# A language-model tower on one core: the output biases from TensorE to VectorE, layer-norm rows among the gelus, one table load taken out, RMS factors five steps earlier

## The chip, the cores and the metric
The kernel runs on one core of a Trainium2 chip. Its time is the device time of one execution, in microseconds (us), as the median of several runs. Engines are named as in the profile: PE (TensorE, matmuls), PEld (its weight loads), DVE (VectorE), ACT (ScalarE), POOL (GpSimd), SP (SyncE, which issues most DMAs).

## The reference
64 sequences of 128 token ids, width 256. Cut to what matters:

```python
h = take(concat(quantize(tw_i * ts_i, bits_i)), ids)          # embedding, four tiers
x = layernorm(h)                                              # attention-like block on x
r = rms(x, norm1_w)
z, u, B, C, dt = split(r @ in_proj_w.T)                       # 512, 512, 16, 16, 8
u, B, C = silu(causal_conv4([u, B, C]) + conv_b)
B, C = B * rsqrt(sum(B*B) + 1e-6), C * rsqrt(sum(C*C) + 1e-6)
d = softplus(dt + dt_bias)
# for t in time: zs = (zs + d*(u*B - A*y)) / (1 + d*d*A); y = y + d*zs; out_t = y . C_t
y = (out + D_skip * u) * silu(z)
x2 = x + y @ out_proj_w.T + out_proj_b                        # first bias of the change
m = gelu(rms(x2, norm2_w) @ fc1_w.T + fc1_b)
h = h + x2 + m @ fc2_w.T + fc2_b                              # second bias of the change
h = h + int8_linear(layernorm(h))                             # one activation scale for all rows
```

## The kernel before
Three blocks follow each other. The first reads the whole table (81 MB) for the tiers' maxima and gathers the rows. The last is the int8 layer. The block between, where the change lies, works on 16 groups of 4 sequences (512 tokens) in 19 turns; turns 4 to 14 are one hardware loop, the others are written out. Each turn holds up to four stages of four different groups: `first` (group g: rows normalised, projected, the small projection of B, C and dt, the recurrence), `second` (group g-1: scores, scan output, gate, out projection), `third` (group g-2: the MLP, gelus 0 to 7) and `fourth` (group g-3: final layer norm and its maximum). The order on each engine is written out by hand in `pe_turn`, `act_turn`, `dve_turn`, `pool_turn`; semaphores join them.

What the steps below touch:
- **POOL** runs the recurrence, 64 steps of two dependent 128x32 instructions (L787, L789). It starts when X, the replicated and scaled d, is there: small projection on PE (L651), exp and ln on ACT (L669, L671), `dd` on DVE (L707), a DMA to memory and eight back (`sp_replicate`), then four activations (L762). Between the steps POOL also makes the norm factors of the next group and, after step `RMS_STEP`, the RMS factors of group g-1 (`pool_rms`, L1047 and L1049). In turn 1 these RMS factors stand behind the last step.
- **ACT** needs those factors for `act_rms_rows` (L1058, buffer xr), PE then transposes (L1064), ACT copies the result out (L1071, mT), and PE begins fc1 (L1091). The first gelu (L1101) lets fc2 (L1113) begin. Before the first gelu ACT has the silus of z (L924), the row copies (L637), the small projection's work with two table loads for exp and ln (L667, L684), and the gelu's own load.
- **PE** adds the biases: `pick` has ones in three rows, `bias3` holds each bias split in three bf16 parts, and a 128x512 bf16 matmul adds them to a bank (L1020 twice per turn ahead of the out projection, L1109 twice ahead of fc2). DVE makes the split in turn 0 (`dve_split_biases`).
- **DVE** after the keys, the inverse (L863) and the queries (L870) applies the masks (L987) to the scores that PE has just made (L976); PE's scan output (L997) waits for them.
- **ACT** makes xl, the layer-normed rows of group g-1 (L955), behind the last gelu and the utok copies (L945). DVE adds the out projection to it (L1032).

Of the kernel before, what the change touches and what calls it, by code (L numbers as in the profile page):

```python
# [36 lines left out]
G = 4  # L37
# [13 lines left out]
RMS_STEP = 52  # L51
# [36 lines left out]
def build(nc, a, out):  # L88
    with ExitStack() as ctx:
# [22 lines left out]
        bias3 = sb("bias3", [P, 2, 2 * D], BF16)  # L112
        pick = sb("pick", [P, P], BF16)
# [42 lines left out]
        LATE_WEIGHTS = ((w_fc1, "w_fc1"), (w_out, "w_out"), (w_fc2, "w_fc2"))  # L156
        OUT_B, FC2_B = 0, 1
# [313 lines left out]
        bias_in, halved, pick_cleared = sem("bias_in"), sem("halved"), sem("pick_cleared")  # L471
# [55 lines left out]
        seeded = signal("seeded", 2)  # L527
        h2_ready = signal("h2_ready", 2)
# [16 lines left out]

        def dve_split_biases(dve):
            whole = utok[:, 0:2, :]
            rest = utok[:, 2:4, :]
            dve.wait_ge(bias_in, 16)
            dve.tensor_copy(bias3[:], whole).then_inc(halved, 1)  # L550
            dve.wait_ge(halved, 1)
            dve.tensor_tensor(rest[64:P], whole[64:P], bias3[64:P], ALU.subtract).then_inc(halved, 1)
            dve.wait_ge(halved, 2)
            dve.tensor_copy(bias3[64:P], rest[64:P]).then_inc(halved, 1)
            dve.wait_ge(halved, 3)
            dve.tensor_tensor(rest[96:P], rest[96:P], bias3[96:P], ALU.subtract).then_inc(halved, 1)
            dve.wait_ge(halved, 4)
            dve.tensor_copy(bias3[96:P], rest[96:P]).then_inc(halved, 1)
# [124 lines left out]
        def act_small_rsqrt(act, g):  # L683
            act.preload_act_table_set("natural_log_exp_and_others")  # L684
            act.wait_ge(nrm_act.sem, nrm_act.at(g, 1))
            act.activation(nrm[:], bsq[:], ACT.Ln).then_inc(nrm_act.sem, 1)
            act.wait_ge(nrm_act.sem, nrm_act.at(g, 2))
            act.activation(nrm[:], nrm[:], ACT.Exp, scale=-0.5).then_inc(nrm_act.sem, 1)
# [268 lines left out]

        score_bank = (tb[0], tb[1], pj[2], pj[3])
# [54 lines left out]
        def pe_out(pe, g):  # L1013
            pe.wait_ge(m_ready.sem, m_ready.at(g))
            if since(g):
                pe.wait_ge(h2_ready.sem, h2_ready.at(g - 1))
            else:
                pe.wait_ge(halved, 5)
            for n in range(2):
                pe.matmul(sbk[n][:, :], pick[:], bias3[:, OUT_B, :], start=True, stop=False, skip_group_check=True)  # L1020
                for j in (2 * n, 2 * n + 1):
                    for f in range(UT):
                        if j == 0:
                            pe.wait_ge(yg_ready.sem, yg_ready.at(g, f + 1))
                        last = pe.matmul(sbk[n][:, (j % 2) * D:(j % 2 + 1) * D], sz[:, f, j * LEN:(j + 1) * LEN],  # L1025
                                         w_out[:, f, :], start=False, stop=(f == UT - 1), skip_group_check=True)
                last.then_inc(o_mm.sem, 1)

        def dve_x2(dve, g, n):
            dve.wait_ge(xl_ready.sem, xl_ready.at(g))  # L1030
            dve.wait_ge(o_mm.sem, o_mm.at(g, n + 1))
            dve.tensor_tensor(xl[:, 2 * n:2 * n + 2, :], sbk[n][:, :].rearrange("p (j c) -> p j c", j=2),  # L1032
                              xl[:, 2 * n:2 * n + 2, :], ALU.add).then_inc(x2_ready.sem, 1)
# [70 lines left out]
        def pe_fc2(pe, g, n):  # L1104

            if n == 0:
                pe.wait_ge(seeded.sem, seeded.at(g))
                for i in range(2):
                    pe.matmul(sbk[i][:, :], pick[:], bias3[:, FC2_B, :], start=False, stop=False,  # L1109
                              skip_group_check=True)  # L1110
# [10 lines left out]
        def dve_h2(dve, g):  # L1121
            for n in range(2):
# [109 lines left out]
        def act_turn(act):  # L1232
            def turn(g, first, second, third, fourth, nxt):
# [7 lines left out]
                if first:  # L1241
                    act_rows_T(act, g)
                if second:
                    act_silu_z(act, p, (3,))
                if third:
                    act_mlp_T(act, m)
# [4 lines left out]
                if first:  # L1251
                    act_small_silu(act, g)
                    act_small_dt(act, g)
                if first:
                    act_small_norm(act, g)
                    act_small_rsqrt(act, g)
                for n in range(FT):
# [6 lines left out]
                    if first and n == 3:  # L1264
                        act_rep(act, g, (1,))
                if second:
                    act_utok(act, p)
                if second:
                    act_layer_norm(act, p)
# [18 lines left out]
        def dve_turn(dve):  # L1288
            def turn(g, first, second, third, fourth, nxt):
# [16 lines left out]
                if not second and nxt:  # L1306
                    dve_bc(dve, g)
                    dve_split_biases(dve)
                    dve_first_steps(dve)
                if second:  # L1310
                    for hh in range(4):
# [31 lines left out]
        def pool_turn(pool):  # L1343
            def turn(g, first, second, third, fourth, nxt):
# [5 lines left out]
                if first and third:  # L1350
# [3 lines left out]
                elif first:  # L1354
                    pool_recurrence(pool, g, range(CL // 2 if second else DVE_STEPS, CL))
                if second and not (first and third):
# [6 lines left out]
        with nc.Block() as block:  # L1363
            @block.sync
            def _(sp):
                sp.dma_start(utok[:, 0:2, :], a["bias"].rearrange("p (i c) -> p i c", i=2)).then_inc(bias_in, 16)

# [21 lines left out]
            def _(dve):  # L1389
# [6 lines left out]
                dve.memset(pick[:], 0.0).then_inc(pick_cleared, 1)  # L1396
                dve.wait_ge(pick_cleared, 1)
                for r in (0, 64, 96):
                    dve.memset(pick[r:r + 1, :], 1.0)
# [313 lines left out]
```

## Time and profile before

| what | value |
|---|---|
| median of 3 runs | 1381.36 us (1380.7 to 1381.74) |
| the profiled execution's own time | 1378.95 us |
| its span, first to last instruction | 1377.1 us |
| busy in the span: PE, DVE, ACT, POOL | 1143.6, 1044.5, 804.8, 780.9 us |
| middle block | from about 175 to 1321 us |
| granted PE clock from 320 to 1223 us | 1.00 of full speed |

The span and the time of the same execution differ by 1.85 us, which lies around the span. In the page's slices PE is 9 tenths busy or more from about 310 us on to 1300 us, while no other engine is. A busy share is no proof of a bound, since PE's idle moments are short and come at fixed places of each turn, so the timelines of one turn are read.

### The profile page before, as it was taken

How to read it: one execution, taken by the hardware profiler on the slowest of the kernel's cores; microseconds unless marked ns; L12 is line 12 of the kernel's file. 1: busy time of each engine (PE TensorE's matmuls, PEld its weight loads, DVE VectorE, ACT ScalarE, POOL GpSimd, SP SyncE). 2: the span in 40 equal slices, each digit the busy share in tenths (PEclk: the TensorE clock that was granted, in tenths of full speed). 3: DMA queues.
4: the chain of work that ended last, by engine and by line, in shares of the span. 5: the costliest groups of instructions: out<-in, count | busy, mean ns of one | idle time of the engine just before them, and what ended most of it. 6: DMA issues, size and time to landing. Idle time of an engine off the chain costs nothing. (4 is left out here: it accounts for less than half of the span.)

```text
span 1377.1 us, 24832 instructions
## 1 busy us (share of the span) xinstructions
PE 1143.6 (83%) x7231; PEld 759.6 (55%) x7270; DVE 1044.5 (76%) x1764; ACT 804.8 (58%) x1288; POOL 780.9 (57%) x2326
## 2 busy tenths in 40 slices
PE   3980032488999999999999999999999999999857
PEld 1550021355766667565757575757666675757534
DVE  5988957756768787877888888887787877786178
ACT  4666433537475756657484847574757566552357
POOL 8880023372757575867667675767575858570000
PEclk9999996588999999999999999999999999999989
DMA  9999610000010000001010101010100000000015
GB/s 367 407 408 410 276 35 15 18 17 19 8 29 15 21 18 17 19 15 29 5 34 0 34 0 34 0 34 6 28 14 20 17 17 20 17 18 2 0 48 197
DMA packets 62082, 92.65 MB, mean 67 GB/s; under 512 B 9101, under 2 KB 54754, under 8 KB 57682
## 3 DMA queue, kind: packets, MB, share of 16 engines
q1 hardware_dynamic: 58386, 82.36, 16.8%
q0 software_dynamic: 3072, 8.39, 1.6%
q10 hardware_dynamic: 576, 1.31, 0.3%
q8 instruction: 23, 0.38, 0.1%
q14 instruction: 25, 0.20, 0.1%
HBM read 81.55 MB, written 10.49 MB: 67 GB/s over the span
## 5 line engine op out<-in xcount | busy, mean ns | idle before, releaser
L787 POOL TENSOR_TENSOR stp<-Gs,X 128x32 f32<-128x32 f32 x984 | 269.8, 274 | 259.0 <-ACT X L762 165.1
L789 POOL TENSOR_TENSOR Gs<-Gs,stp 128x32 f32<-128x32 f32 x984 | 274.3, 279 | 77.0
L641 PE MATMUL bank<-xT,w_in 128*128 128x512 f32 x512 | 239.8, 613 | 26.6 <-DVE uT L899 26.6
L1113 PE MATMUL bank<-w_fc,gl 128*128 128x256 f32 x1024 | 244.5, 382 | 10.7 <-ACT gl L1101 10.7
L1091 PE MATMUL bank<-mT,w_fc 128*128 128x512 f32 x512 | 238.7, 600 | 7.3 <-ACT mT L1071 7.3
L1113 PEld LDWEIGHTS bank<-w_fc,gl 128*128 128x128 f32 x1024 | 189.8, 190 | 69.5 <-issue 26.8
L641 PEld LDWEIGHTS bank<-xT,w_in 128*128 128x128 f32 x512 | 96.1, 195 | 129.5 <-issue 97.0
L885 ACT ACTIVATE uT<-bank,cols 128x512 f32<-128x512 f32 x64 | 47.9, 775 | 190.4 <-DVE sz L1011 155.1
L1091 PEld LDWEIGHTS bank<-mT,w_fc 128*128 128x128 f32 x512 | 95.8, 192 | 93.6 <-issue 86.9
L987 DVE TENSOR_TENSOR MT<-bank,causal 128x512 f32<-128x512 f32 x128 | 79.4, 682 | 85.4 <-PE bank L976 85.4
L1101 ACT ACTIVATE gl<-bank,cols 128x512 f32<-128x512 f32 x128 | 84.2, 682 | 98.9 <-PE bank L1113 94.2
L899 DVE SCALAR_TENSOR_TENSOR uT<-bank,cols,uT 128x500 f32<-128x500 f32 (+1 forms) x192 | 133.3, 735 | 2.3
L346 DVE TENSOR_TENSOR peak<-ring,peak 128x1536 f32<-128x1536 f32 (+2 forms) x67 | 115.2, 1720 | 7.9 <-ACT ring L248 6.2
L248 ACT ACTIVATE ring<-ring 128x3072 f32<-128x3072 f32 (+4 forms) x36 | 90.7, 2530 | 49.9 <-DMA ring<-in_table 49.9
L1025 PE MATMUL bank<-w_out,sz 128*128 128x256 f32 x512 | 116.5, 381 | 1.1 <-issue 0.3
L1025 PEld LDWEIGHTS bank<-w_out,sz 128*128 128x128 f32 x512 | 98.0, 191 | 19.5 <-issue 5.0
L863 DVE RECIPROCAL rm<-rm 128x1024 f32<-128x1024 f32 x16 | 104.7, 6543 | 0.0
L232 POOL DMA_INDIRECT h<-in_table,ids x64 | 82.0, 1281 | 19.4 <-issue 19.4
L762 ACT ACTIVATE X<-d_rep,cols 128x512 f32<-128x512 f32 x64 | 72.6, 1187 | 27.8 <-DMA d_rep<-d_rows 27.8
L286 PE MATMUL bank<-ts,hot 4*128 4x256 f32 x128 | 60.3, 648 | 19.6 <-ACT hot L259 14.1
L695 DVE SCALAR_TENSOR_TENSOR bc<-bank,cols,bc 128x127 f32<-128x127 f32 (+2 forms) x48 | 16.7, 348 | 72.4 <-ACT bc L661 71.3
L976 PE MATMUL bank<-Qf,Kf 32*128 32x64 f32 x2048 | 67.8, 282 | 3.1 <-DVE Qf L870 3.1
(184 smaller groups left out, 1868.5 us busy)
## 6 DMA issues: line engine op xcount, KB each, us to landing
ring<-in_table SPq DMA_DIRECT2D x31, 1536.0 KB
d_rep<-d_rows SPq DMA_DIRECT2D x128, 64.0 KB, 2.7
out<-res SPq DMA_DIRECT2D x16, 512.0 KB, 2.9
b_rep<-bc_rows SPq DMA_DIRECT2D x128, 32.0 KB, 1.8
c_rep<-bc_rows SPq DMA_DIRECT2D x128, 32.0 KB, 1.8
w_fc<-in_w_fc SPq DMA_DIRECT2D x2, 1024.0 KB, 8.8
ring<-in_table SPq DMA_DIRECT2D x2, 768.0 KB
w_in<-in_w_in ACTq DMA_DIRECT2D x1, 1088.0 KB
```

The source lines that it names most:

```text
L232: pool.indirect_dma_start(out=h[:, b * D:(b + 1) * D], out_offset=None, in_=table, in_offset=bass.IndirectOffsetOnAxis(ap=ids[:, b:b + 1], ...
L248: act.activation(ring[n % RING][0:np_, 0:nr, :], ring[n % RING][0:np_, 0:nr, :], ACT.Abs) \
L346: return dve.tensor_tensor(acc, ring[t][0:np_, r0:r0 + nr, :], acc, ALU.max)
L641: last = pe.matmul(dst, w_in[:, k, c0:c1], xT[:, k, :], start=(k == 0), stop=(k == KD - 1))
L787: pool.tensor_tensor(stp[:], Gs[:, t, ::-1, :], X2[:, t, :, :], ALU.mult).then_inc(rec.sem, 1)
L789: pool.tensor_tensor(Gs[:, t + 1, :, :], Gs[:, t, :, :], stp[:], ALU.add).then_inc(rec.sem, 1)
L863: dve.reciprocal(rm[:], rm[:]).then_inc(inverted.sem, 1)
L899: dve.scalar_tensor_tensor(acc[:, :, i:], ps[:, :, 0:LEN - i], c("u_tap", f * TAPS + TAPS - 1 - i), acc[:, :, i:], ALU.mult, ALU.add).then ...
L1025: last = pe.matmul(sbk[n][:, (j % 2) * D:(j % 2 + 1) * D], sz[:, f, j * LEN:(j + 1) * LEN], w_out[:, f, :], start=False, stop=(f == UT - 1 ...
L1091: last = pe.matmul(pj[n % 4][:, :], w_fc1[:, k, n * P:(n + 1) * P], mT[:, k, :], start=(k == 0), stop=(k == KD - 1))
L1101: act.activation(gl[n % LEAD][:], pj[n % 4][:, :], ACT.Gelu_apprx_tanh, bias=c("fc1_bias", n)) \
L1113: last = pe.matmul(sbk[j // 2][:, (j % 2) * D:(j % 2 + 1) * D], gl[n % LEAD][:, j * LEN:(j + 1) * LEN], w_fc2[:, n, :], start=False, stop= ...
```

## The change
The bias matmuls, `pick`, `bias3` and `dve_split_biases` go. Both biases are now loaded as [128, 256] float32 tiles with the late weights, and DVE adds them once per group, broadcast over the 4 sequences: out_proj_b to xl and fc2_b to h (`dve_biases`), ahead of the masks. On ACT the layer-norm rows stand behind gelu 5, the mT copies ahead of the last z silu, and the second load of the exp and ln table is left out where `first` and `third` both run; where only `first` runs, exp and ln of dt come ahead of the silu of B and C. On POOL `RMS_STEP` is 47, and turn 1 too has its RMS factors inside the recurrence.

```diff
-RMS_STEP = 52
+RMS_STEP = 47
-        bias3 = sb("bias3", [P, 2, 2 * D], BF16)
-        pick = sb("pick", [P, P], BF16)
+        out_b = sb("out_b", [P, D])
+        fc2_b = sb("fc2_b", [P, D])
-        LATE_WEIGHTS = ((w_fc1, "w_fc1"), (w_out, "w_out"), (w_fc2, "w_fc2"))
+        LATE_WEIGHTS = ((w_fc1, "w_fc1"), (w_out, "w_out"), (w_fc2, "w_fc2"), (out_b, "out_b"), (fc2_b, "fc2_b"))
@@ act_small_rsqrt
-            act.preload_act_table_set("natural_log_exp_and_others")
+        def dve_biases(dve, g):
+            dve.wait_ge(xl_ready.sem, xl_ready.at(g))
+            dve.tensor_tensor(xl[:], xl[:], out_b[:].unsqueeze(1).to_broadcast([P, G, D]), ALU.add) \
+                .then_inc(biased.sem, 1)
+            dve.tensor_tensor(rows(g, 0, G).rearrange("p (j c) -> p j c", j=G),
+                              rows(g, 0, G).rearrange("p (j c) -> p j c", j=G),
+                              fc2_b[:].unsqueeze(1).to_broadcast([P, G, D]), ALU.add).then_inc(biased.sem, 1)
@@ pe_out
-                pe.matmul(sbk[n][:, :], pick[:], bias3[:, OUT_B, :], start=True, stop=False, skip_group_check=True)
-                                         w_out[:, f, :], start=False, stop=(f == UT - 1), skip_group_check=True)
+                                         w_out[:, f, :], start=(f == 0), stop=(f == UT - 1))
@@ dve_x2
-            dve.wait_ge(xl_ready.sem, xl_ready.at(g))
+            dve.wait_ge(biased.sem, biased.at(g, 1))
@@ pe_fc2
-                for i in range(2):
-                    pe.matmul(sbk[i][:, :], pick[:], bias3[:, FC2_B, :], start=False, stop=False,
-                              skip_group_check=True)
@@ act_turn
+                if third:
+                    act_mlp_T(act, m)
                 if second:
                     act_silu_z(act, p, (3,))
-                if third:
-                    act_mlp_T(act, m)
...
-                if first:
+                if first and third:
                     act_small_silu(act, g)
                     act_small_dt(act, g)
-                if first:
                     act_small_norm(act, g)
                     act_small_rsqrt(act, g)
+                elif first:
+                    act_small_dt(act, g)
+                    act_small_silu(act, g)
+                    act_small_norm(act, g)
+                    act.preload_act_table_set("natural_log_exp_and_others")
+                    act_small_rsqrt(act, g)
                 for n in range(FT):
...
+                    if second and n == 5:
+                        act_layer_norm(act, p)
                 if second:
                     act_utok(act, p)
-                if second:
-                    act_layer_norm(act, p)
@@ dve_turn
-                    dve_split_biases(dve)
                     dve_first_steps(dve)
                 if second:
+                    dve_biases(dve, p)
                     for hh in range(4):
                         dve_mask(dve, p, 0, hh)
@@ pool_turn
-                if first and third:
+                if first and second:
                     pool_recurrence(pool, g, range(CL // 2, RMS_STEP))
                     pool_rms(pool, p)
                     pool_recurrence(pool, g, range(RMS_STEP, CL))
@@ the first instructions of DVE in the middle block
-                dve.memset(pick[:], 0.0).then_inc(pick_cleared, 1)
-                dve.wait_ge(pick_cleared, 1)
-                for r in (0, 64, 96):
-                    dve.memset(pick[r:r + 1, :], 1.0)
```

On ACT, in turn 2 (the first with all of the stages up to the MLP), before: from the copy of the norm sums to the last gelus (bsq and nrm belong to B and C's norms, X is the scaled d, gl the gelus, utok here the squares, xl the layer-norm rows).

```order
L681 ACTIVATE bsq<-bank,cols 128x128
L684 ACT_TABLE_LOAD
L686 ACTIVATE nrm<-bsq 128x128
L688 ACTIVATE nrm<-nrm 128x128
L1101 ACT_TABLE_LOAD
L1101 ACTIVATE gl<-bank,cols 128x512
L805 ACTIVATE utok<-Gs 128x2048
L1101 ACTIVATE gl<-bank,cols 128x512 x2
L762 ACTIVATE X<-d_rep,cols 128x64x8 x2
L1101 ACTIVATE gl<-bank,cols 128x512
L762 ACTIVATE X<-d_rep,cols 128x64x8 x2
L1101 ACTIVATE gl<-bank,cols 128x512 x4
```

The same place now.

```order
L666 ACTIVATE bsq<-bank,cols 128x128
L670 ACTIVATE nrm<-bsq 128x128
L672 ACTIVATE nrm<-nrm 128x128
L1090 ACT_TABLE_LOAD
L1090 ACTIVATE gl<-bank,cols 128x512
L789 ACTIVATE utok<-Gs 128x2048
L1090 ACTIVATE gl<-bank,cols 128x512 x2
L746 ACTIVATE X<-d_rep,cols 128x64x8 x2
L1090 ACTIVATE gl<-bank,cols 128x512
L746 ACTIVATE X<-d_rep,cols 128x64x8 x2
L1090 ACTIVATE gl<-bank,cols 128x512 x2
L939 ACTIVATE xl<-h,off,rs 128x256 x4
```

The second table load has gone, and the four xl rows have come behind gelu 5, ahead of gelus 6 and 7.

On DVE, in turn 2, before: from the inverse to the first masks (rm the inverse, Qf the queries, MT the masked scores).

```order
L863 RECIPROCAL rm<-rm 128x1024
L870 SCALAR_TENSOR_TENSOR Qf<-rm,Qf 128x512 x2
L574 BN_STATS st<-h 128x6 x4
L577 BN_AGGR mv<-st 128x2 x4
L987 TENSOR_TENSOR MT<-bank,causal 128x512 x4
```

The same place now.

```order
L847 RECIPROCAL rm<-rm 128x1024
L854 SCALAR_TENSOR_TENSOR Qf<-rm,Qf 128x512 x2
L559 BN_STATS st<-h 128x6 x4
L562 BN_AGGR mv<-st 128x2 x4
L944 TENSOR_TENSOR xl<-xl,out_b 128x1024
L946 TENSOR_TENSOR h<-h,fc_b 128x1024
L979 TENSOR_TENSOR MT<-bank,causal 128x512 x4
```

Two adds of 1024 elements stand between the statistics and the masks.

On ACT, in turn 0, before: the small projection (bc holds B and C).

```order
L675 ACT_TABLE_LOAD
L675 ACTIVATE bc<-bc 128x128
L677 ACTIVATE bsq<-bc 128x128
L667 ACT_TABLE_LOAD
L669 ACTIVATE soft<-soft 128x128
L671 ACTIVATE soft<-soft 128x128
L681 ACTIVATE bsq<-bank,cols 128x128
L684 ACT_TABLE_LOAD
```

The same place now.

```order
L652 ACT_TABLE_LOAD
L654 ACTIVATE soft<-soft 128x128
L656 ACTIVATE soft<-soft 128x128
L660 ACT_TABLE_LOAD
L660 ACTIVATE bc<-bc 128x128
L662 ACTIVATE bsq<-bc 128x128
L666 ACTIVATE bsq<-bank,cols 128x128
L1247 ACT_TABLE_LOAD
```

Exp and ln of dt have come ahead of the silu of bc and its table load. In turn 1, where the silu's table is there already when the small projection begins, the same order now has three loads in place of two.

## Rows read from the trace of the kernel before
**Rows 1.** Timeline of PE, turn from 900 us: start, length, engine, line, [idle <-releaser].
```profile
900.51 1.09 PE L1064 MATMUL bank<-ident,xr 128*128 128x128 f32 x8 [0.21 <-ACT xr L1058]
...
903.49 3.69 PE L1091 MATMUL bank<-mT,w_fc 128*128 128x512 f32 x8 [0.46 <-ACT mT L1071]
...
912.03 1.99 PE L1113 MATMUL bank<-w_fc,gl 128*128 128x256 f32 x8 [0.76 <-ACT gl L1101]
...
936.80 1.97 PE L997 MATMUL bank<-MT,utok 128*64 128x128 f32 x32
...
953.43 0.38 PE L1020 MATMUL bank<-bias,pick 128*128 128x512 bf16 x1
953.64 3.62 PE L1025 MATMUL bank<-w_out,sz 128*128 128x256 f32 x16
```

**Rows 2.** Timeline of PE: fc2's start in turn 2 and in turn 15.
```profile
326.62 1.99 PE L1113 MATMUL bank<-w_fc,gl 128*128 128x256 f32 x8 [0.68 <-ACT gl L1101]
...
1171.34 1.99 PE L1113 MATMUL bank<-w_fc,gl 128*128 128x256 f32 x8 [0.84 <-ACT gl L1101]
```

**Rows 3.** Timeline of ACT, turn from 900 us.
```profile
908.04 1.28 ACT L684 ACT_TABLE_LOAD   x1
...
911.29 0.69 ACT L1101 ACTIVATE gl<-bank,cols 128x512 f32<-128x512 f32 x1
911.88 1.90 ACT L805 ACTIVATE utok<-Gs 128x2048 f32<-128x2048 f32 x1
...
924.40 0.69 ACT L1101 ACTIVATE gl<-bank,cols 128x512 f32<-128x512 f32 x1 [2.21 <-PE bank L1113]
...
931.85 2.07 ACT L955 ACTIVATE xl<-h,off,rs 128x256 f32 x4
...
963.78 1.71 ACT L1058 ACTIVATE xr<-xl,ssq 128x256 f32<-128x256 f32 x4 [2.45 <-POOL ssq L1049]
```

**Rows 4.** Timeline of POOL, the same turn.
```profile
905.17 0.96 POOL L787 TENSOR_TENSOR stp<-Gs,X 128x32 f32<-128x32 f32 x1
906.21 0.95 POOL L789 TENSOR_TENSOR Gs<-Gs,stp 128x32 f32<-128x32 f32 x1
...
921.12 0.25 POOL L787 TENSOR_TENSOR stp<-Gs,X 128x32 f32<-128x32 f32 x1 [8.88 <-ACT X L762]
921.45 0.25 POOL L789 TENSOR_TENSOR Gs<-Gs,stp 128x32 f32<-128x32 f32 x1
```

**Rows 5.** Timeline of DVE, the same turn.
```profile
904.84 2.20 DVE L773 SCALAR_TENSOR_TENSOR bk<-X,cols,b_rep 128x512 f32<-128x512 f32 x2
...
908.16 1.12 DVE L822 TENSOR_TENSOR Kf<-bk,Gs 128x512 f32<-128x512 f32 x1
...
913.81 1.22 DVE L833 TENSOR_TENSOR rm<-utok 128x1024 f32<-128x1024 f32 x1 [1.59 <-ACT utok L805]
...
935.11 2.48 DVE L987 TENSOR_TENSOR MT<-bank,causal 128x512 f32<-128x512 f32 x4 [4.48 <-PE bank L976]
```

**Rows 6.** Timeline of DVE from 176 us: pick, turn 0, turn 1.
```profile
176.02 0.62 DVE L1399 MEMSET pick<- 1x128 bf16 x3
...
210.13 0.19 DVE L796 TENSOR_TENSOR stp<-Gs,X 128x32 f32<-128x32 f32 x1 [4.33 <-ACT X L762]
...
270.69 2.48 DVE L987 TENSOR_TENSOR MT<-bank,causal 128x512 f32<-128x512 f32 x4 [1.02 <-PE bank L976]
```

**Rows 7.** Timeline of ACT in turns 0 and 1.
```profile
193.80 1.28 ACT L675 ACT_TABLE_LOAD   x1
...
195.76 1.28 ACT L667 ACT_TABLE_LOAD   x1
...
300.05 0.19 ACT L1041 ACTIVATION_READ_ACCUMULATOR gl<-xl 128x1 f32 x1
```

**Rows 8.** Timeline of POOL in turn 1: where the row factors stand.
```profile
310.79 0.20 POOL L1047 TENSOR_TENSOR ssq<-ssq,eps 128x4 f32<-128x4 f32 x1
```

**Rows 9.** Timeline of PE: transposes at the start of turn 2's MLP.
```profile
313.87 1.97 PE L1064 MATMUL bank<-ident,xr 128*128 128x128 f32 x8 [7.63 <-ACT xr L1058]
```

More of the change, by code:

```diff
@@ L154, in build @@
         tok_step = sem("tok_step")
-        LATE_WEIGHTS = ((w_fc1, "w_fc1"), (w_out, "w_out"), (w_fc2, "w_fc2"))
-        OUT_B, FC2_B = 0, 1
+        LATE_WEIGHTS = ((w_fc1, "w_fc1"), (w_out, "w_out"), (w_fc2, "w_fc2"), (out_b, "out_b"), (fc2_b, "fc2_b"))
         def rows(g, j=0, n=1):
@@ L470, in build @@
         begun = sem("begun")
-        bias_in, halved, pick_cleared = sem("bias_in"), sem("halved"), sem("pick_cleared")
         quant = signal("quant", 2 * G)
@@ L527, in build @@
         seeded = signal("seeded", 2)
+        biased = signal("biased", 2)
         h2_ready = signal("h2_ready", 2)
@@ L542, in chunks @@
             return ap.rearrange("p (s t) -> p t s", t=CL)
[L546 to L558, printed above, removed]
         def dve_quantise(dve, g):
@@ L1016, in pe_out @@
                 pe.wait_ge(h2_ready.sem, h2_ready.at(g - 1))
-            else:
-                pe.wait_ge(halved, 5)
             for n in range(2):
-                pe.matmul(sbk[n][:, :], pick[:], bias3[:, OUT_B, :], start=True, stop=False, skip_group_check=True)
                 for j in (2 * n, 2 * n + 1):
@@ L1121, in dve_h2 @@
         def dve_h2(dve, g):
+            dve.wait_ge(biased.sem, biased.at(g))
             for n in range(2):
@@ L1354, in turn @@
                 elif first:
-                    pool_recurrence(pool, g, range(CL // 2 if second else DVE_STEPS, CL))
-                if second and not (first and third):
+                    pool_recurrence(pool, g, range(DVE_STEPS, CL))
+                elif second:
                     pool_rms(pool, p)
@@ L1365, in _ @@
             def _(sp):
-                sp.dma_start(utok[:, 0:2, :], a["bias"].rearrange("p (i c) -> p i c", i=2)).then_inc(bias_in, 16)
                 def turn(g, first, second, third, fourth, nxt):
@@ L1702 @@
         "w_q": wide(f["L0_ffn_weight_int8"].T).view(np.int32),
-        "bias": rows(np.concatenate([f[f"L0_attn_{n}"] for n in ("out_proj_b", "out_proj_b", "fc2_b", "fc2_b")])),
+        "out_b": rows(f["L0_attn_out_proj_b"]),
+        "fc2_b": rows(f["L0_attn_fc2_b"]),
         "q_cols": np.stack([tall(f["L0_ffn_weight_scale"]), tall(f["L0_ffn_bias"])], axis=1),
```

## The prediction
> **What bounds the kernel now.** I read the timeline of one middle turn engine by engine, then the first turns. PE first [rows 1]. The z projection ends at 900.51 - 0.21 = 900.30, and PE then waits at four places: 0.21 us for the RMS rows xr, a short wait for xT, 0.46 for mT, 0.76 for the first gelu. From fc2's start at 912.03 on it runs without a gap to the next such point. So PE's turn is its work plus waits that all lie in its first 12 us. Thirteen turns, from the fc2 start at 326.62 to that at 1171.34 [rows 2], took 844.72 us, 64.98 each.
>
> ACT next [rows 3]. It gives xr late because POOL does: at 963.78 it has waited 2.45 us for the RMS factors, and xr ends at 965.49. ACT's work from there to the first gelu has no wait worth naming, two loads of the same table in it. POOL last [rows 4]: it idled 8.88 us before its recurrence, which starts at 921.12 when X is there. X in turn hangs on the small projection, that is on the same xr end through ACT's queue. So two loops are nearly equal: PE's own, and **xr end, small projection, d, X, 52 recurrence steps, RMS factors, xr end**, which has the last word, since PE waits for xr by 0.21 us here.
>
> **The POOL loop, part by part.** A step is two instructions 0.33 us apart (921.12 and 921.45) [rows 4], 0.66 us. RMS_STEP 47 takes out five: -3.30. The bias adds lie inside it. Each is an add of 1024 float32 from SBUF; the nearest row is 1.22 us (913.81, [rows 5]), so 2.45 for both. What this does to POOL is read from the pair of bk operations: 2.20 us on DVE from 904.84 on [rows 5], and beside them two POOL instructions of 0.96 and 0.95 in place of 0.25 [rows 4], a loss of 1.41, 0.64 per us of DVE. Times 2.45: +1.6. The bounds are no collision, 0, and POOL stopped for all of it, 2.45; I take 1.6 since bk too is an operation with two SBUF inputs. The loop becomes 64.98 - 3.30 + 1.6 = **63.3**.
>
> The Trainium skill speaks against this part: "SBUF — State Buffer", section "Who interferes with whom", says that a VectorE instruction with two SBUF inputs holds a read port that GpSimd needs, and that the later one stands still for the whole instruction. The rows agree in kind, less in size. By that rule POOL would lose the adds' whole 2.45; rival 2 works that case out from rows.
>
> **The PE loop.** This turn was short, 64.70 by the xr wait being 0.21 only; without that wait PE's work and its own waits make 64.49. Removed: two bias matmuls ahead of the out projection, each 0.21 to 0.22 (953.43 to 953.64) [rows 1], -0.43. The two ahead of fc2 save nothing by themselves here: the 0.76 wait for the gelu stands behind them and takes their place. But the gelu comes sooner. The second table load is 1.28 (908.04, [rows 3]) on ACT's unbroken run to gelu 0, so fc2 may begin 1.28 earlier, and PE's work allows that (0.76 + 0.43 + what mT gives). The mT copies ahead of the last silu give PE 0.46, which matters only behind the first limit. PE loop: 64.49 - 0.43 - 1.28 = **62.8**. It stays under 63.3, so POOL decides, by 0.5.
>
> **What is moved.** The xl rows cost ACT 2.07 us wherever they are [rows 3]. Behind gelu 5 they meet an idle 2.21 ahead of gelu 6 (924.40), and gelus 6 and 7 are not needed by fc2 until three slots later: 0. If that cover went, DVE's bias adds would start late, as priced next. **The masks** have DVE idle 4.48 before them [rows 5]. The adds take 2.45 of it and PE's earlier scores 1.28, which leaves 0.75. The keys (908.16) begin later against PE, by the 1.6 that POOL lost and the 1.7 that the turn is shorter, less the 1.59 that the chain waited for ACT's squares at 913.81: 1.7 at most. So the masks can be 0.95 late; PE's scan output has a slack of 936.80 - 935.11 less two masks (half of 2.48), 0.45. The stall is at most 0.5, and 62.8 + 0.5 is still 63.3. I count 0. Queued behind the adds on DVE are the masks, h2, the skips and gates, then the convolutions; they moved with PE before and do so now.
>
> Per turn 64.98 - 63.3 = 1.7, times 13: **-22.1**.
>
> **The first turns.** Four pick memsets, three of them 0.62 us (176.02, [rows 6]), stand on DVE ahead of the first normalisation, which everything waits for; with about 0.2 for the fourth and its semaphore, -0.8. In turn 0 dt's table load can start at 193.80 and not 195.76 [rows 7], so d, its DMAs, X and the 40 steps on DVE come 2.0 sooner. The bias split itself saves nothing: DVE waited 4.33 for X behind it [rows 6]. In turn 1 the order costs a third load ahead of the squares, 1.28, and the inverse and queries follow them. The scores then come later by as much, so the adds, 2.45, still have only 1.02 of idle to hide in (270.69, [rows 6]): 1.28 + 1.43 = +2.7, less 0.43 of matmuls. Sum to the end of z in turn 2: -0.8 - 2.0 + 2.7 - 0.4 = -0.5.
>
> There PE waited 7.63 us for xr [rows 9], because the RMS factors stood behind step 64, at 310.79 [rows 8]. Seventeen steps earlier is 299.6; the sums are there at 300.24 [rows 7]. Factors and xr then end near 304, and z ends at 313.87 - 7.63 - 0.5 = 305.7. The wait is gone: -7.6. From transpose to fc2 took 12.75 us here (326.62 less 313.87), after an idle stretch and with transposes at 1.97 for eight against 1.09 in the steady turn; steady and without the load it is 10.4: -2.3. Together -0.5 - 7.6 - 2.3 = **-10.4**.
>
> **The end.** From the fc2 start at 1171.34 on, the pairs of bias matmuls in turns 15 (out), 16 (fc2 and out) and 17 (fc2) lie between dense matmuls: 4 x 0.43 = **-1.7**. The two bias tiles, 256 KB, come behind the late weights in the first block, whose end DVE's maxima set, not these DMAs: 0.
>
> **Sum.** 1378.95 - 10.4 - 22.1 - 1.7 = 1344.7 for the profiled execution's own time (span 1377.1 and 1.85 around it). The median lies 2.4 above that execution, so 1347.1.
>
> **Rivals.**
> 1. *PE's loop decides.* If the adds cost POOL under 1.1, xr is early and the turn is 62.8: 13 x 0.5 = 6.5 less, 1340.5. For: POOL's own pieces under single adds lose less than their whole length. Against: the bk rows. Chance 0.15.
> 2. *The port is held whole.* POOL loses 2.45, the turn is 64.98 - 3.30 + 2.45 = 64.1: 13 x 0.85 = 11 more, 1358. For: an instruction of 0.96 beside an operation of 1.1 looks like one that was stopped, not slowed. Against: the pair as a whole, 0.64 per us. Chance 0.18. (The Trainium skill's page named above states this case.)
> 3. *The turn does not shorten.* Something stands where the loads and steps were, such as the squares waiting for the recurrence and holding gelu 1: only the ends gain, 1347 + 22 = 1369. For: squares (911.88) wait for the recurrence and block the gelus behind them. Against: PE has a piece of fc1 and one of fc2 to do between needing gelu 0 and gelu 1. Chance 0.09.
> 4. *Slower: the adds and POOL collide both ways.* Each add waits for POOL's instructions as POOL waits for it, 4.9 us for both on DVE and on POOL. The loop becomes 64.98 - 3.3 + 4.9 = 66.6, +1.6 per turn, +21 - 12.1 = +9, 1390. It decides from a loss of 4.3 on. For: the shared steps do stretch each other. Against: in the one collision of the rows DVE's pair took 2.20 in all, while POOL lost 1.41. Chance 0.04.
> The forecast keeps 0.54.
>
> **Range and chances.** The costs' bounds (0 to 2.45 on POOL, the PE loop as floor, about 3 us either way in the first turns) give 1338 to 1361. That leaves out rivals 3 and 4, 0.13. A change under 0.2% (2.8 us) cannot be told from none. Faster 0.94, same 0.02, slower 0.04.
>
> **What would show it.** Right: turns of 63.3 us; POOL's two steps beside the bias adds near 1 us; xr ending just behind z; one exp load per turn; no xr wait in turn 2; fc2 about 10.4 behind the transposes. Wrong: DVE's idle time before the masks gone and PE waiting at the scan output, or PE waiting for xr by more than 1 us.

## The result and the profile after

| | before | after |
|---|---|---|
| median of 4 runs | 1381.55 us (1380.7 to 1382.56) | 1356.13 us (1355.13 to 1358.38) |
| ratio | | 0.9814, 95% interval 0.9802 to 0.9826 |
| the profiled execution's own time | 1378.95 us | 1358.38 us |

The kernel is 25.4 us faster. The forecast of 1347.1 us was 9 us too low, and the time lies inside its range, next to the 1358 us of rival 2. Taken apart by the same marks as in the prediction, the two profiled executions differ like this:

| stretch | predicted, us | measured, us |
|---|---|---|
| to the fc2 start of turn 2 (326.62, now 314.75) | -10.4 | -11.9 |
| thirteen turns, to the fc2 start of turn 15 (1171.34, now 1150.10) | -22.1 | -9.4 |
| from there to the end | -1.7 | +0.7 |
| sum | -34.2 | -20.6 |

The profiled execution of after is the slowest of its four; that of before lies under all four of its column, which is why the medians differ by more than the profiles. The miss is in the thirteen turns: 835.35 us / 13 = 64.26 us each, where 63.3 was forecast and 64.98 was before.

PE in the timeline of after (start, length, engine, line; in brackets the idle time before it and who ended it), to be held against [rows 1], [rows 2] and [rows 9]:

```profile
304.51 1.04 PE L1053 MATMUL bank<-ident,xr 128*128 128x128 f32 x8
...
314.75 1.97 PE L1099 MATMUL bank<-w_fc,gl 128*128 128x256 f32 x8 [0.54 <-ACT gl L1090]
...
883.86 1.09 PE L1053 MATMUL bank<-ident,xr 128*128 128x128 f32 x8 [1.26 <-ACT xr L1047]
...
894.12 1.99 PE L1099 MATMUL bank<-w_fc,gl 128*128 128x256 f32 x8 [0.40 <-ACT gl L1090]
...
919.26 2.29 PE L989 MATMUL bank<-MT,utok 128*64 128x128 f32 x32 [0.30 <-DVE MT L979]
...
947.40 1.09 PE L1053 MATMUL bank<-ident,xr 128*128 128x128 f32 x8
...
1150.10 1.97 PE L1099 MATMUL bank<-w_fc,gl 128*128 128x256 f32 x8 [0.54 <-ACT gl L1090]
```

Three things are to be seen. The wait of 7.63 us in turn 2 is gone. From turn 3 to turn 15 PE waits for xr in nine turns of thirteen, by 1.07 to 1.56 us (1.26 at 883.86), and not in the other four (947.40). Of the twelve turns between, the eight that end in such a wait last 64.5 to 64.9 us, the others 63.4 to 63.9. And the scan output (L989), which waited for nothing before, now waits for the masks.

POOL is busy for 841.7 us of the span with 2326 instructions, where the same number took 780.9 before.

POOL in the timeline of after, against [rows 4]:

```profile
904.57 0.71 POOL L771 TENSOR_TENSOR stp<-Gs,X 128x32 f32<-128x32 f32 x1 [4.46 <-ACT X L746]
...
915.82 1.11 POOL L773 TENSOR_TENSOR Gs<-Gs,stp 128x32 f32<-128x32 f32 x1
917.01 1.11 POOL L771 TENSOR_TENSOR stp<-Gs,X 128x32 f32<-128x32 f32 x1
918.20 0.25 POOL L773 TENSOR_TENSOR Gs<-Gs,stp 128x32 f32<-128x32 f32 x1
...
944.13 0.20 POOL L1036 TENSOR_TENSOR ssq<-ssq,eps 128x4 f32<-128x4 f32 x1
...
967.92 0.88 POOL L771 TENSOR_TENSOR stp<-Gs,X 128x32 f32<-128x32 f32 x1 [4.00 <-ACT X L746]
...
979.02 1.37 POOL L771 TENSOR_TENSOR stp<-Gs,X 128x32 f32<-128x32 f32 x1
980.47 1.11 POOL L773 TENSOR_TENSOR Gs<-Gs,stp 128x32 f32<-128x32 f32 x1
```

DVE in the timeline of after, against [rows 5] and [rows 6]:

```profile
208.17 0.19 DVE L780 TENSOR_TENSOR stp<-Gs,X 128x32 f32<-128x32 f32 x1 [5.97 <-ACT X L746]
...
904.17 1.03 DVE L844 TENSOR_TENSOR Kf<-bk,utok 128x512 f32<-128x512 f32 x1
...
915.55 1.26 DVE L944 TENSOR_TENSOR xl<-xl,out_b 128x1024 f32<-128x1024 f32 x1
916.74 1.27 DVE L946 TENSOR_TENSOR h<-h,fc_b 128x1024 f32 x1
917.93 2.47 DVE L979 TENSOR_TENSOR MT<-bank,causal 128x512 f32<-128x512 f32 x4
```

Beside each add one POOL instruction lasts until the add ends: 915.82 + 1.11 = 916.93 beside an add that ends at 916.81, and 917.01 + 1.11 = 918.12 beside one that ends at 918.01. Both lost 1.11 - 0.25 = 0.86, so 1.72 in this turn; in the next, 1.12 + 0.86 = 1.98. The masks beside POOL's next instructions cost it nothing (0.25 at 918.20): they too write a full tile to SBUF, but one of their two inputs is a PSUM bank. One more place takes from POOL. Its recurrence now begins while DVE still makes the last keys (0.71 at 904.57 beside L844; before, it began at 0.25, [rows 4]). And before the masks DVE has no idle time any more, where it had 4.48 [rows 5]. From the recurrence's start to the RMS factors POOL needs 944.13 - 904.57 = 39.56 us in this turn, and 40.6 to 40.7 in most of the others.

ACT in the timeline of after, against [rows 3]: the first gelu's load follows the small projection at once, and xr waits for POOL's factors in every turn from 3 to 15, by 1.8 to 3.2 us. The copy of B and C starts 4.48 us behind xr in each of these turns, and 4.47 before, so PE holds nothing up on this path: the POOL loop closes in every turn, also in those in which PE does not wait.

```profile
882.10 1.71 ACT L1047 ACTIVATE xr<-xl,ssq 128x256 f32<-128x256 f32 x4 [3.17 <-POOL ssq L1038]
...
892.08 1.28 ACT L1090 ACT_TABLE_LOAD   x1
...
905.54 2.06 ACT L939 ACTIVATE xl<-h,off,rs 128x256 f32 x4
...
945.64 1.71 ACT L1047 ACTIVATE xr<-xl,ssq 128x256 f32<-128x256 f32 x4 [1.96 <-POOL ssq L1038]
```

### The profile page after: what moved, and what is told of

Its sections match the earlier page's. It is cut to its first block and busy times, and to the rows that moved or that the text cites. A ratio compares the mean times of both kernels' runs of the same rounds, so it can differ in the third digit from the quotient of the medians.

```text
span 1356.3 us, 24768 instructions
## 1 busy us (share of the span) xinstructions
PE 1132.9 (84%) x7199; PEld 752.4 (55%) x7206; DVE 1075.5 (79%) x1787; ACT 786.7 (58%) x1275; POOL 841.7 (62%) x2326
## 5 line engine op out<-in xcount | busy, mean ns | idle before, releaser
L771 POOL TENSOR_TENSOR stp<-Gs,X 128x32 f32<-128x32 f32 x984 | 299.6, 304 | 181.1 <-ACT X L746 83.9
L773 POOL TENSOR_TENSOR Gs<-Gs,stp 128x32 f32<-128x32 f32 x984 | 291.2, 296 | 77.2
L1014 PE MATMUL bank<-w_out,sz 128*128 128x256 f32 x512 | 113.7, 380 | 0.4 <-DVE sz L1003 0.4
L989 PE MATMUL bank<-MT,utok 128*64 128x128 f32 x1024 | 69.0, 286 | 9.2 <-DVE MT L979 7.9
L989 PEld LDWEIGHTS bank<-MT,utok 128*64 128x64 f32 x1024 | 58.0, 142 | 29.6 <-DVE MT L979 17.3
```

The source lines that it names most:

```text
L771: pool.tensor_tensor(stp[:], Gs[:, t, ::-1, :], X2[:, t, :, :], ALU.mult).then_inc(rec.sem, 1)
L773: pool.tensor_tensor(Gs[:, t + 1, :, :], Gs[:, t, :, :], stp[:], ALU.add).then_inc(rec.sem, 1)
L989: last = pe.matmul(pj[head // 2][64 * (head % 2):64 * (head % 2) + 64, j * LEN:(j + 1) * LEN], utok[:, j, head * HP:(head + 1) * HP], MT[h ...
```

## The experiments

The theory after the result: POOL's loop decides, as forecast, but the adds cost it more than 1.6 us, since they block its reads until they end; through the later keys they also make the masks late. The rival: the adds' own length on DVE is the price. "Turn" below is the mean of twelve distances between the starts of the MLP's transposes on PE, turn 3 to turn 15, in the profiled execution; by it before is 64.95 and after 64.28.

| kernel | turn, us | median, us | ratio to before, 95% interval |
|---|---|---|---|
| POOL's part alone | 64.30 | 1360.65 | 0.9847 (0.9832 to 0.9862) |
| ACT's part alone | 65.37 | 1381.34 | 1.0002 (0.9989 to 1.0015) |
| POOL's and ACT's part, biases on PE | 63.02 | 1339.32 | 0.9709 (0.969 to 0.9728) |
| the same, step 44 | 63.06 | 1341.16 | 0.9718 (0.9696 to 0.9739) |
| after (all three parts) | 64.28 | 1356.13 | 0.9814 (0.9802 to 0.9826) |
| after, step 44 | 63.52 | 1351.64 | 0.9782 (0.9756 to 0.9807) |
| after, step 52 | 67.95 | 1411.4 | 1.0207 (1.0163 to 1.0251) |
| after, table load back | 63.99 | 1356.53 | 0.9804 (0.9773 to 0.9835) |
| after, no adds, no biases | 62.59 | 1331.79 | 0.9641 (0.9614 to 0.9668) |
| after, reductions for adds | 62.67 | 1334.82 | 0.9668 (0.9639 to 0.9697) |
| after, one-tensor operations for adds | 62.67 | 1334.38 | 0.9668 (0.9652 to 0.9684) |
| after, second add late | 63.87 | 1352.5 | 0.979 (0.9754 to 0.9825) |
| after, second add late, step 44 | 64.50 | 1355.86 | 0.9808 (0.9767 to 0.985) |

### What of the adds costs: none, reductions, one-tensor operations

No adds: both operations of `dve_biases` and the waits for them are left out, and with them the biases.

```diff
                 if second:
-                    dve_biases(dve, p)
```

> The two adds are left out, and so are the biases. Theory A: no port taken and no late masks: PE's loop without its stall at the scan output, 62.8 us per turn, 13 x 1.45 = 19 less, and 1.4 in turn 1: 1335 us. Theory B: the same, 1335 us; both say it, and it gives the price of the adds as a whole. If turns stay above 63.5, a loop that neither theory has decides.

Reductions: two operations of about the same length that read one tensor each and write 4 numbers per partition.

```diff
-            dve.tensor_tensor(xl[:], xl[:], out_b[:]..., ALU.add)
-            dve.tensor_tensor(rows(g, 0, G)..., rows(g, 0, G)..., fc2_b[:]..., ALU.add)
+            dve.tensor_reduce(scr0[:], xl[:], AX.X, ALU.max, apply_absolute_value=True)
+            dve.tensor_reduce(scr1[:], rows(g, 0, G)..., AX.X, ALU.max, apply_absolute_value=True)
```

> The two adds are replaced by two maximum reductions over the same 1024 elements, with one SBUF input each, so the biases are left out, and DVE is busy for the same 2.4 us. Theory A: what the adds cost is the SBUF port they share with POOL. POOL's two stretched steps are 0.25 us each, the POOL loop falls by 1.9 to about 62.4, turns are 63.2 to 63.5 us by PE's loop, 1343 us. Theory B (DVE's own time makes the masks late): turns stay at 64.3, 1356 us.

One-tensor operations: the full tile is read and written, in place, with one number per partition added.

```diff
+            dve.tensor_scalar(xl[:], xl[:], out_b[:, 0:1], None, ALU.add)
+            dve.tensor_scalar(rows(g, 0, G)..., rows(g, 0, G)..., fc2_b[:, 0:1], None, ALU.add)
```

> The changed kernel with each of the two adds made an operation of one tensor operand and one number per partition (the first column of the bias is added to all), over the same 1024 elements, read and written in place: the rest of the bias is left out. Theory A (what the adds cost GpSimd is the second tensor operand, as the reductions of the same length suggest): GpSimd's rows beside them stay at 0.25 us, 1335 us. Theory B (it is the writing of the full tile in place, which the reductions did not have): as the changed kernel, 1356 us.

Measured: 1331.79, 1334.82 and 1334.38 us. Timelines of DVE and of POOL with the reductions:

```profile
958.05 1.19 DVE L946 TENSOR_REDUCE scr<-xl 128x4 f32<-128x1024 f32 x1
959.16 1.21 DVE L947 TENSOR_REDUCE scr<-h 128x4 f32 x1
```

```profile
958.31 0.25 POOL L773 TENSOR_TENSOR stp<-Gs,X 128x32 f32<-128x32 f32 x1
...
959.63 0.25 POOL L773 TENSOR_TENSOR stp<-Gs,X 128x32 f32<-128x32 f32 x1
```

And with the one-tensor operations:

```profile
956.26 0.73 DVE L944 TENSOR_SCALAR xl<-xl,out_b 128x1024 f32<-128x1024 f32 x1
956.91 0.74 DVE L945 TENSOR_SCALAR h<-h,fc_b  x1
```

```profile
956.52 0.58 POOL L773 TENSOR_TENSOR Gs<-Gs,stp 128x32 f32<-128x32 f32 x1
957.17 0.59 POOL L771 TENSOR_TENSOR stp<-Gs,X 128x32 f32<-128x32 f32 x1
```

With DVE as busy as with the adds (two times 1.2 us), POOL keeps its 0.25 and the kernel gets within about 3 us of the one without adds. So the 21 to 24 us are not DVE's time: the rival falls. The one-tensor operations miss a part of both expectations: they ran in 0.73 us and not in the adds' 1.25, so they are no pair of equal length, and POOL lost 0.33 and 0.34 beside them, not nothing. The turn is still 62.6, since PE's loop decides there. Without adds every turn is PE's own work and waits, 62.59 us; the prediction had 62.8.

The Trainium skill ("SBUF — State Buffer", section "Who interferes with whom") tells the three cases apart: two SBUF inputs hold the port that GpSimd reads by, a reduction or an operation with one SBUF input does not, and a tensor_scalar that runs in a two-port mode does; the waiting engine stops and is not slowed. The rows agree with each of the three (1.11, 0.25 and 0.58 in place of 0.25); that the tensor_scalar ran in such a mode is seen here only by its 0.73 us. They also show what the rule makes of a time, which I had not worked out: POOL's instruction ends about 0.1 us behind DVE's. What POOL loses is then the length of DVE's operation less the part of it in which POOL's instruction was still free to run: 0.40 less where the add began beside a running instruction (1.26 and 0.86; 0.73 and 0.33), 0.07 less where it began just ahead of one (1.19 and 1.12, the add beside 979.02).

### Which loop decides: POOL's part alone, ACT's part alone, step 52

POOL's part alone:

```diff
-RMS_STEP = 52
+RMS_STEP = 47
-                if first and third:
+                if first and second:
                     pool_recurrence(pool, g, range(CL // 2, RMS_STEP))
                     pool_rms(pool, p)
```

> The kernel before with only GpSimd's part of the change: the RMS factors behind step 47 instead of 52, and in the second turn inside the recurrence too; biases by TensorE, two table loads and the order of ScalarE as before. If two loops bound the turn as the prediction has it (GpSimd's 64.98 us less 3.30, TensorE's 64.49 us), TensorE's takes over at 64.49 us a turn: 13 x 0.49 = 6 us less, and 7.6 us of the wait in the third turn go: 1368 us. If GpSimd's loop never decided, the turn stays at 64.98 us and only the third turn's wait goes: 1374 us. If TensorE's loop falls with it: under 1360 us.

ACT's part alone is `act_turn` and `act_small_rsqrt` of the change in the kernel before:

```diff
         def act_small_rsqrt(act, g):
-            act.preload_act_table_set("natural_log_exp_and_others")
...
+                    if second and n == 5:
+                        act_layer_norm(act, p)
```

> The kernel before with only ScalarE's part of the change: one table load less, the layer norm rows among the gelus, the order of the first turns; RMS factors behind step 52 and biases on TensorE as before. Theory A (GpSimd's loop decides before): the turn stays at 64.98 us and the load brings nothing: 1376 to 1381 us, the difference only in the first turns. Theory B (the load of 1.28 us lies on the path): 13 x 1.28 = 16.6 us less, 1364 us.

The changed kernel with the old step:

```diff
-RMS_STEP = 47
+RMS_STEP = 52
```

> The changed kernel with the RMS factors behind step 52, as before. Theory A (GpSimd's loop decides, and the adds cost it 1.7 to 2.0 us a turn): the loop is 64.98 + 1.8 = 66.8 us, 2.5 us over the changed kernel's 64.26, and the recurrence ends later for the first turns too: 1356 + 13 x 2.5 = 1389 us, slower than the kernel before. Theory B (GpSimd's loop has slack and the late masks on VectorE decide): about 1356 to 1365 us.

Measured 1360.65, 1381.34 and 1411.4 us. ACT's part alone brings nothing: with POOL's loop in charge at 64.9 us, the table load that it saves comes back as a longer wait for xr (1.72 us a turn in the later turns, 0.54 before). Its mean turn is longer by 0.4, since turns 3 to 7 took 65.6 to 67.0; the first turns, 3.6 shorter together, make up for a part of it. POOL's part alone brings 20.6 us, more than the 14 that I expected; of its profiled execution, 1362.15 us, the 16.8 less than before are 7.6 in turn 2 and 13 x 0.67 = 8.7 in the turns, and the other 3.8 lie between executions. Its PE rows show turns of exactly 64.3 us without a wait for xr, and the first gelu's wait as before:

```profile
884.95 1.04 PE L1064 MATMUL bank<-ident,xr 128*128 128x128 f32 x8
...
896.46 1.99 PE L1113 MATMUL bank<-w_fc,gl 128*128 128x256 f32 x8 [0.76 <-ACT gl L1101]
...
949.27 1.04 PE L1064 MATMUL bank<-ident,xr 128*128 128x128 f32 x8
```

So PE's loop before was 64.3, not the 64.49 that I took.

The changed kernel with step 52 is 30 us slower than before, and 22 us slower than theory A had it. It differs from "ACT's part alone" only in the biases and in turn 1's factors, and both are bound by POOL's loop. PE waits for xr by 3.2 to 4.4 us in its later turns. In the mean the turn stands at 67.95 against 65.37, 2.6 more. Their timelines of POOL, first ACT's part alone:

```profile
727.26 0.25 POOL L785 TENSOR_TENSOR stp<-Gs,X 128x32 f32<-128x32 f32 x1 [9.80 <-ACT X L760]
...
768.25 0.20 POOL L1045 TENSOR_TENSOR ssq<-ssq,eps 128x4 f32<-128x4 f32 x1
```

Then the changed kernel with step 52:

```profile
734.25 0.25 POOL L771 TENSOR_TENSOR stp<-Gs,X 128x32 f32<-128x32 f32 x1 [8.81 <-ACT X L746]
...
742.78 1.11 POOL L771 TENSOR_TENSOR stp<-Gs,X 128x32 f32<-128x32 f32 x1
743.97 1.11 POOL L773 TENSOR_TENSOR Gs<-Gs,stp 128x32 f32<-128x32 f32 x1
...
776.61 0.25 POOL L1036 TENSOR_TENSOR ssq<-ssq,eps 128x4 f32<-128x4 f32 x1
```

From the recurrence's start to the factors: 768.25 - 727.26 = 40.99 and 776.61 - 734.25 = 42.36 us in these turns, 1.4 more, of which the adds' two rows hold 1.72 (other collisions give a little back). That is not the whole difference of the turn. The rest is on PE. PE and ACT in the same turn, first ACT's part alone:

```profile
706.75 1.09 PE L1062 MATMUL bank<-ident,xr 128*128 128x128 f32 x8 [1.08 <-ACT xr L1056]
708.19 1.08 PE L650 MATMUL bank<-xT,w_in 128*32 128x128 f32 x32 [0.35 <-ACT xT L636]
```

```profile
709.46 0.49 ACT L660 ACTIVATE bc<-bank,cols 128x128 f32<-128x128 f32 x1
```

Then the changed kernel with step 52:

```profile
712.76 1.97 PE L1053 MATMUL bank<-ident,xr 128*128 128x128 f32 x8 [4.41 <-ACT xr L1047]
714.66 1.75 PE L636 MATMUL bank<-xT,w_in 128*32 128x128 f32 x32
```

```profile
716.49 0.46 ACT L646 ACTIVATE bc<-bank,cols 128x128 f32<-128x128 f32 x1 [0.64 <-PE bank L636]
```

After the long wait PE's transposes take 1.97 us and not 1.09, and the small projection 1.75 and not 1.08: in the same place of a later turn, from 984 to 988 us, the granted clock is 0.50 of full speed, its lower level (1.2 GHz), after 3.44 us of idle time. In the changed kernel, whose waits are 1.1 to 1.6 us, it is 1.00. ACT then waits 0.64 us for the small projection, which lies in POOL's loop: from xr's start to the copy of B and C 5.49 us go by (711.00 to 716.49), not 4.47 (704.99 to 709.46). So a wait that POOL's loop causes on PE makes that same loop longer. The means over turns 4 to 14, from the profiled executions:

| kernel | steps | xr's start to B and C's copy, us | recurrence's start to factors, us |
|---|---|---|---|
| before | 52 | 4.47 | 40.97 |
| ACT's part alone | 52 | 4.59 | 41.06 |
| after, step 52 | 52 | 5.54 | 42.75 |
| after | 47 | 4.48 | 40.31 |
| after, no adds, no biases | 47 | 4.92 | 38.29 |

In the last row PE's loop decides and holds the copy back. By the table **the adds cost POOL 1.7 us a turn with step 52 and 2.0 us in the changed kernel**, where the prediction had 1.6; the other 0.95 of the 2.6 in the step 52 kernel is PE's lower clock, which neither theory had. Theory A's 66.8 us and this 1.0 give 67.8, and 67.95 was measured. That 67.6, the last turns' length, less 3.30 for five steps gives the changed kernel's 64.3 is an accident, since that kernel has no such loss of clock. That its turn is POOL's rests on ACT's rows above.

### The table load

```diff
                     act_small_norm(act, g)
+                    act.preload_act_table_set("natural_log_exp_and_others")
                     act_small_rsqrt(act, g)
```

> The second load of the exp and ln table is back in every turn from 2 to 15. Theory A: it lies in PE's loop (63.5 + 1.28 = 64.8) and not in POOL's (64.3), so turns become 64.8 and only 0.5 per turn is lost: 1356 + 7 = 1363 us. Rival: the load is on the one path that decides, 14 x 1.28 = 18, 1374 us.

Measured 1356.53 us against 1356.13 of the changed kernel: no difference, both expectations missed. PE in its timeline:

```profile
881.78 1.04 PE L1053 MATMUL bank<-ident,xr 128*128 128x128 f32 x8
...
893.29 1.99 PE L1099 MATMUL bank<-w_fc,gl 128*128 128x256 f32 x8 [1.68 <-ACT gl L1090]
...
918.06 1.97 PE L989 MATMUL bank<-MT,utok 128*64 128x128 f32 x32
...
945.66 1.04 PE L1053 MATMUL bank<-ident,xr 128*128 128x128 f32 x8
```

The load is on PE's path: the wait for the gelu is 0.40 + 1.28 = 1.68. But the masks are then in time (918.06, no wait), and xr too; the turn is 63.88, the 62.59 of the kernel without adds and 1.28. Taking the load out turns that wait into one for the masks and one for xr. The mean turn with the load is even 0.3 us shorter than without it (63.99 and 64.28), so in the changed kernel the removal of the load gained nothing by itself.

### The biases on PE again, all else as in the change

```diff
+                pe.matmul(sbk[n][:, :], pick[:], bias3[:, OUT_B, :], start=True, stop=False, skip_group_check=True)
...
+                for i in range(2):
+                    pe.matmul(sbk[i][:, :], pick[:], bias3[:, FC2_B, :], start=False, stop=False, ...)
...
-                    dve_biases(dve, p)
```

> The changed kernel with the biases on TensorE as before (bias3, pick and the four matmuls a turn), and all the rest of the change: RMS factors behind step 47 and in the second turn inside the recurrence, one table load less, layer norm rows among the gelus. Theory A (the adds load GpSimd's loop by 2.6 us a turn, and that loop decides the changed kernel): GpSimd's loop is 64.98 - 3.30 = 61.7 us, TensorE's 64.31 (measured with GpSimd's part alone) less one load of 1.28 = 63.0 us, which decides: 13 x (64.26 - 63.0) = 16 us less than the changed kernel, 1340 us; with what the adds cost the first turns, 1336 us. Theory B (the changed kernel is bound by something that stays, and moving the biases helped as it was meant to): 1356 us plus the matmuls, 13 x 0.43 = 1362 us.

> The kernel with the biases on TensorE, with the RMS factors behind step 44 instead of 47. Theory A (its GpSimd loop, 61.7 us, has slack under TensorE's 63.03): no change, 1338 to 1341 us, turns at 63.0 us. Theory B (GpSimd's loop still decides some turns): faster by up to 13 x 0.5 = 6 us, 1333 us.

Measured 1339.32 us, and 1341.16 with step 44, no difference that the intervals can tell. This kernel beats both others: 42 us under the kernel before, 17 under the changed one. Timeline of PE:

```profile
868.16 1.04 PE L1062 MATMUL bank<-ident,xr 128*128 128x128 f32 x8
...
903.16 1.97 PE L995 MATMUL bank<-MT,utok 128*64 128x128 f32 x32
...
931.19 1.04 PE L1062 MATMUL bank<-ident,xr 128*128 128x128 f32 x8
```

Timeline of DVE:

```profile
901.47 2.48 DVE L985 TENSOR_TENSOR MT<-bank,causal 128x512 f32<-128x512 f32 x4 [2.45 <-PE bank L974]
```

931.19 - 868.16 = 63.03: PE waits for neither xr nor the masks, DVE has 2.45 us idle before these, and here the table load is worth its whole 1.28 (64.30 to 63.02). The bias matmuls cost 63.02 - 62.59 = 0.43 us a turn, as the prediction had it. PE holds back the copy of B and C here (5.4 us behind xr's start, not 4.5), so POOL's loop has slack. That the matmuls cost less than what the adds take from POOL and PE is the finding of this study: **the bias part of the change lost 17 us of what its two other parts gained.**

### The masks, and moving an add

Step 44 in the changed kernel:

```diff
-RMS_STEP = 47
+RMS_STEP = 44
```

> RMS factors after step 44 instead of 47. Theory A (two loops: POOL's, from xr over X and the recurrence to the RMS factors, 64.3 us per turn with the adds in it, and PE's own, 63.5): the POOL loop falls by 2.0, PE's loop decides, turns of 63.5 to 63.6 us, 1346 us; PE no longer waits for xr. The sums of squares are ready 2.4 us before the factors now, so POOL does not wait for them. Theory B (DVE's late masks set the turn, the xr wait is only where PE's spare time shows): turns stay at 64.3, 1356 us.

Measured 1351.64 us (1343.68 to 1352.97); the profiled execution is its fastest. PE in its timeline:

```profile
907.65 2.29 PE L989 MATMUL bank<-MT,utok 128*64 128x128 f32 x32 [0.77 <-DVE MT L979]
...
935.57 1.04 PE L1053 MATMUL bank<-ident,xr 128*128 128x128 f32 x8
```

No turn waits for xr now, and the turn stands at 63.5, not at 62.6: what is left is the stall at the masks, up to 0.77 us idle and 0.32 more in the matmuls that follow, and in two turns of twelve, this one among them, 0.59 us for a later gelu. So the late masks are the second cost of the adds, behind POOL's loop. This holds for the profiled execution; the median lies 8 us above it, and where those 8 us go was not seen.

The second add moved to behind the next quantising, then with step 44 too:

```diff
                     dve_quantise(dve, g + 1)
+                if third:
+                    dve_bias_h(dve, m)
                 if first:
                     dve_conv_small(dve, g)
```

> The changed kernel with the second add (fc2's bias, 1.23 us) moved on VectorE from ahead of the masks to behind the next quantising, where VectorE has about 2 us idle and GpSimd is past the step that makes the RMS factors. Theory A (the add costs through the port that it shares with GpSimd's recurrence, and through the masks behind it): the 0.86 us that this add takes from the recurrence goes, and the masks start 1.2 us sooner: turns at 63.2 to 63.4 us instead of 64.26, 1344 us. Theory B (the price is VectorE's own length, and moved it delays the convolution and the gated factors that GpSimd's next recurrence waits for): 1354 to 1360 us.

> The same, with the RMS factors behind step 44 instead of 47. Theory A: GpSimd's loop falls under TensorE's 62.58 us, and the turn stands at TensorE's: 13 x 1.7 = 22 us less than the changed kernel, 1335 us, as without the adds at all. Theory B: no better than step 44 with both adds ahead of the masks, 1350 us.

Measured 1352.5 us (1347.02 to 1358.21) and 1355.86 (1347.35 to 1361.55), with intervals that overlap that of the changed kernel: the first lies between the two theories and is inconclusive, the second is a clear miss of theory A's 1335. I had looked at where POOL makes its factors and had overlooked that it goes on with steps 44 to 64, so the moved add met it again. What POOL and PE wait for, from 700 to 955 us, with step 44 (in total, times, longest), the waits of POOL:

```profile
POOL stp L772 <- DVE utok L841: 22.0, 4, 5.8
```

The waits of PE:

```profile
PE bank L1103 <- ACT gl L1094: 7.4, 7, 1.9
```

This is a third loop, of 64.8 us in the profiled execution: all 64 steps, the keys that DVE makes from Gs, and the next recurrence, which may write Gs only behind them. Its end also holds the squares on ACT, and these the gelus behind them, the mechanism that rival 3 named.

## Why the prediction was right, and where its size was off

- **Sign, place and mechanism: right.** Two loops nearly equal, POOL's in charge, PE's next. ACT's part alone (nothing), POOL's part alone (20.6 us, PE's loop at 64.3) and step 52 (67.95) show it.
- **The signs.** Of the signs of being right, POOL's two steps near 1 us (1.11), the missing wait in turn 2 and fc2 10.2 us behind the transposes came; the turn of 63.3 did not. Both signs of being wrong came too: no idle time before the masks with PE waiting at the scan output (0.30), and PE waiting for xr by more than 1 us (1.26). They mark the sizes below and not another mechanism.
- **The mis-sized term: "+1.6" for the adds in POOL's loop.** The changed kernel's turn is POOL's loop throughout, so the term is 64.26 - (64.98 - 3.30) = 2.6. The stretch from the recurrence's start to the factors says the same: 40.31 against 40.97 - 3.30 = 37.67. Of this, 2.0 goes with the adds (40.31 against 38.29 without them): their own rows hold 1.72 or 1.98, 1.9 in the mean, where the scaling by 0.64 per us of the bk pair gave 1.6. The other 0.6 (38.29 against 37.67) is there without adds. The recurrence now starts earlier against DVE (POOL idles 4.0 to 4.5 us ahead of it, 8.8 to 10.2 before), and without adds it already loses 0.3 of the 0.6 beside the last keys; where the rest goes was not worked out. The prediction left POOL's meetings with DVE as they were before. 13 x 1.0 = 13 us, all of the miss in the turns. Rival 2 had 64.1 us a turn and 1358 us, with a chance of 0.18. Its reason, a port held until the operation ends, is what the rows show; its number came out by luck in part, since it has 2.45 for rows that lost 1.9.
- **"The stall is at most 0.5 ... I count 0": wrong in size.** At 919.26 it is 0.30 idle plus 2.29 against 1.97. Against the kernel without adds PE there falls 0.70 us behind, and PE's loop is 63.3 to 63.5, not 62.8. In the changed kernel that is hidden beside POOL's 64.3; it shows with step 44.
- **PE's loop of 62.8: right but for the masks.** 62.59 without adds. The load's 1.28 and the matmuls' 0.43 are there to the hundredth once POOL has slack.
- **First turns, -10.4: measured -11.9.** DVE's first step moved from 210.13 to 208.17, the 2.0 of turn 0. The pick memsets' 0.8 did not show: the first table load of turn 0 is at 193.77 and was at 193.80 [rows 7]. Turn 1 cost less than forecast, so that z ends 1.7 sooner, not 0.5; the 7.6 us wait went whole, and transposes to fc2 take 10.2 us as forecast (10.4).
- **The end, -1.7: measured +0.7.** The stretch to turn 17's transposes got 0.5 shorter (1257.31 - 1150.10 against 1279.02 - 1171.34), and what follows 1.1 longer. The cause of the latter stays open.
- **Layer norm behind gelu 5, and mT: 0, right.** They show as no wait. What they are worth alone was not measured.

## What to carry to other kernels

Price work that is moved to VectorE by what it does to GpSimd beside it: here an operation with two SBUF inputs stopped GpSimd until it ended (0.86 or 1.12 us lost per add), and one with a PSUM input or a reduction did not. Then look at what the move shifts against what: 0.6 of the missed 1.0 us a turn is there without the adds too. And a wait that grows on TensorE can cost its clock, and with it more than the wait. Half a microsecond of matmul can be the cheaper place for a bias. When two loops are within a microsecond, test each part of a change alone and in pairs: here ScalarE's part was worth nothing alone and 21 us once GpSimd's was in (1360.65 to 1339.32).

## What was not expected of the hardware

- After TensorE had waited 3.2 to 4.4 us for xr (step 52), the granted clock fell to 0.50, eight transposes took 1.97 us in place of 1.09, and the loop that had caused the wait became 1.0 us longer. Over the four executions the granted clock is 0.936 to 0.948, where ScalarE's part alone has 0.959 to 0.965, and the two slowest of them have the lowest.
- A reduction of 1024 elements and an add of the same length (1.2 us each) differ by 21 us in the kernel's time, with the same place and the same waits.
- A one-tensor tensor_scalar over 1024 float32 in SBUF took 0.73 us where a reduction took 1.2, and took 0.33 from POOL; POOL's 0.25 is untouched beside masks of two inputs, one of which is in PSUM.
- Some kernels with both adds scatter more: 1343.7 to 1353.0 us with step 44 and 1347.0 to 1358.2 with the late add, against 1338.2 to 1341.3 with the biases on PE; the changed kernel itself does not (1355.1 to 1358.4). The profile of one execution is then a weak witness for the median. Why they scatter was not settled.
